# Splitting each projection and FFN matmul into two 64-row halves that sum outside TensorE

## The reference

```python
# attention half (16 heads of 64; Wf is 64x64)
n = LN(x)
q, k, v = n @ Wq, n @ Wk, n @ Wv
qf, kf = relu(q @ Wf + bf), relu(k @ Wf + bf)        # per head
kv, k_sum = einsum('blhf,blhd->bhfd', kf, v), kf.sum(axis=1)
out = einsum('blhf,bhfd->blhd', qf, kv) / maximum(einsum('blhf,bhf->blh', qf, k_sum), 1e-6)
x = x + LN(out @ Wo + bo)
# FFN half (1024 -> 4096 -> 4096 -> 4096 -> 1024, ternary weights, a scale per output row)
n = LN(x)
h = silu(n @ w1.T * s1) * (n @ w2.T * s2)
h = gelu(h @ h1.T * sh1)
h = gelu(h @ h2.T * sh2)
x = x + LN(h @ w3.T * s3)
```

## Time and profile before

| what | value |
|---|---|
| median of 3 runs | 8166.21 us (8165.4 to 8902.82) |
| profiled execution, its own time | 8160.16 us |
| span of the profiled execution, slowest of 8 cores | 8158.5 us (cores: 8137.2 to 8158.5) |
| mean granted TensorE clock, by core | 0.848 to 0.850 |
| TensorE matmuls busy | 5912.7 us (72%), 26064 instructions |
| TensorE weight loads busy | 2567.9 us (31%) |
| VectorE busy | 1504.9 us (18%) |
| ScalarE busy | 1102.5 us (14%) |
| chain that ended last, by engine | PE 69%, DVE 15%, DMA 8%, ACT 4%, issue 3% |

### The profile page before, as it was taken

How to read it: one execution, slowest core, us unless ns; L and a number is a source line. 1 busy time by engine, 2 the same in 40 slices (tenths; PEclk the granted TensorE clock), 3 DMA queues, 4 the chain that set the end, 5 groups by cost and what they waited for, 6 DMA issues and landing times.

```text
span 8158.5 us, 65823 instructions; the slowest of 8 cores (8137.2 to 8158.5 us)
## 1 busy us (share of the span) xinstructions
PE 5912.7 (72%) x26064; PEld 2567.9 (31%) x26064; DVE 1504.9 (18%) x1968; ACT 1102.5 (14%) x1781; POOL 214.0 (3%) x392
## 2 busy tenths in 40 slices
PE   3433336799996679999734333368999967799996
PEld 1211112344442334444312111123444423344442
DVE  2355541000002100000133555410000021000002
ACT  1221111110101111001112211111101011100011
POOL 0000000000000000000000000000000000000000
PEclk7666668899998889999866666688999978899998
DMA  3121102244443224344331211022444432344442
GB/s 68 31 57 31 36 26 48 56 78 75 75 78 85 55 57 78 73 77 78 72 78 31 57 32 36 26 52 56 75 77 78 79 91 44 60 78 73 77 78 78
DMA packets 106236, 507.70 MB, mean 62 GB/s; under 512 B 7568, under 2 KB 24016, under 8 KB 56784
## 3 DMA queue, kind: packets, MB, share of 16 engines
q0 software_dynamic: 76368, 402.82, 26.9%
q1 hardware_dynamic: 29568, 100.67, 3.4%
HBM read 864.23 MB, written 41.94 MB: 111 GB/s over the span
## 4 chain that ended last, share of the span: by engine, by line
PE 69%; DVE 15%; DMA 8%; ACT 4%; issue 3%; DVEq 0%; POOL 0%; ACTq 0%; SPq 0%; POOLq 0%
PE psb L56 69%; DMA wc<-w_t 5%; DVE ltmp L75 5%; DVE normsb L103 3%; DVE xa L75 2%; DVE vsb L103 2%; ACT sq L64 1%; DMA xbf<-x 1%; ACT kftm L64 1%; ACT z L64 1%; DVE xp L75 1%; DVE outt L75 1%; DVE rbc L96 1%; DVE y L75 1%; DMA xnw<-xn_hbm 0%
## 5 line engine op out<-in xcount | busy, mean ns | idle before, releaser
L56 PE MATMUL psb<-a,wc 128*128 128x512 bf16 x10240 | 2225.2, 381 | 47.8 <-DMA wc<-h_t 35.0
L56 PE MATMUL psb<-b,wc 128*128 128x512 bf16 x8192 | 1768.7, 379 | 4.8 <-ACT b L64 4.8
L56 PEld LDWEIGHTS psb<-a,wc 128*128 128x128 bf16 x10240 | 1004.2, 98 | 1268.7 <-issue 70.7
L56 PE MATMUL psb<-xnw,wc 128*128 128x512 bf16 x4096 | 963.2, 401 | 503.1 <-DMA wc<-w_t 388.1
L56 PEld LDWEIGHTS psb<-b,wc 128*128 128x128 bf16 x8192 | 801.3, 98 | 972.3 <-issue 6.7
L96 DVE COPY msb<-psb 1x512 f32<-1x512 f32 x40 | 27.1, 679 | 4609.7 <-PE psb L56 4553.4
L56 PEld LDWEIGHTS psb<-xnw,wc 128*128 128x128 bf16 x4096 | 416.1, 102 | 1051.8 <-issue 618.6
L89 DVE SCALAR_TENSOR_TENSOR a<-psb,s,ltmp 128x512 bf16<-128x512 f32 x256 | 192.2, 751 | 1214.0 <-PE psb L56 1195.0
L56 PE MATMUL psb<-xa,WA 128*128 128x512 bf16 x1024 | 251.9, 412 | 208.1 <-DVE xa L75 208.1
L64 ACT ACTIVATE a<-psb,sh 128x512 bf16<-128x512 f32 x256 | 175.9, 687 | 1597.7 <-PE psb L56 1597.7
L64 ACT ACTIVATE b<-psb,sh 128x512 bf16<-128x512 f32 x256 | 175.9, 687 | 1562.0 <-PE psb L56 1561.9
(11 more groups left out here) (79 smaller groups left out, 2324.2 us busy)
## 6 DMA issues: line engine op xcount, KB each, us to landing
wc<-h_t POOLq DMA_DIRECT2D x256, 1024.0 KB, 7.9
wc<-w_t POOLq DMA_DIRECT2D x96, 1024.0 KB, 9.4
xb<-x SPq DMA_DIRECT2D x16, 2048.0 KB, 9.8
xbf<-x POOLq DMA_DIRECT2D x16, 1024.0 KB, 8.9
xp_hbm<-xp SPq DMA_DIRECT2D x8, 2048.0 KB, 9.8
xpr<-xp_hbm SPq DMA_DIRECT2D x8, 2048.0 KB, 15.2
out<-outt SPq DMA_DIRECT2D x8, 2048.0 KB, 7.3
xn_hbm<-xa SPq DMA_DIRECT2D x8, 1024.0 KB, 3.9
```

What stands on the lines that cost most here:

```text
L56: ins = self.h.matmul(out, lhsT, rhs, start=start, stop=stop)
```

## The change

A new helper `mm2` issues two matmuls in place of one: rows 0 to 63 of the weights and of the moving data into one bank, with the array position (0, 0), and rows 64 to 127 into another bank, with the position (64, 0). It replaces `mm` in all projections (K, V, Q, output, W1, W2, H1, H2, W3). Each group of accumulating matmuls then leaves two partial sums in two banks (A and B), which are added on the way out: ACT copies bank A into a scratch tile in SBUF, DVE adds bank B to it. A new 128 x 512 float32 scratch tile `ltmp3` is placed, and the arena grows from 202 to 206 KB; all 8 banks serve as pairs. New waits keep the single scratch tiles from being overwritten (`st["l3_ve"]`, `st["ltmp_ve"]`), TensorE waits for DVE in place of ACT after K and Q, and `ln_fm` gets a wait for DVE on its source.

```diff
+    def mm2(self, outA, outB, lhsT, rhs, start, stop, sem=None):
+        ins = None
+        if self.E == "T":
+            self.h.matmul(outA, lhsT[0:64, :], rhs[0:64, :], start=start,
+                          stop=stop, tile_position=(0, 0))
+            ins = self.h.matmul(outB, lhsT[64:128, :], rhs[64:128, :], start=start,
+                                stop=stop, tile_position=(64, 0))
         self._inc(ins, sem, 1)
...
# K projection (the Q projection alike, V with its own views)
-            p.act(kql[oc], ps[bk][:, :], AF.Copy)
-            bank_consumed(bk, "se")
+            p.w("S", "ve", st["l3_ve"])
+            p.act(t["ltmp3"][:, :], ps[bA][:, :], AF.Identity)
+            bank_consumed(bA, "se")
+            se_i = p.c["se"]
+            p.w("V", "se", se_i)
+            p.tt(kql[oc], t["ltmp3"][:, :], ps[bB][:, :], ALU.add)
+            st["l3_ve"] = p.c["ve"]
+            bank_consumed(bB)
         se_k = p.c["se"]
+        ve_k = p.c["ve"]
+        p.w("T", "ve", ve_k)
...
# output projection
-            p.act(zl[oc], ps[bk][:, :], AF.Identity, bias=t["bo_t"][:, oc:oc + 1])
-            p.act(t["sq"][:, oc * TT:(oc + 1) * TT], ps[bk][:, :], AF.Square,
+            p.w("S", "ve", st["l3_ve"])
+            p.act(t["ltmp3"][:, :], ps[bA][:, :], AF.Identity,
                   bias=t["bo_t"][:, oc:oc + 1])
...
+            p.tt(zl[oc], t["ltmp3"][:, :], ps[bB][:, :], ALU.add)
...
+            p.w("S", "ve", ve_z)
+            p.act(t["sq"][:, oc * TT:(oc + 1) * TT], zl[oc], AF.Square)
...
# W1/W2 stage, one group
-                bw1 = h
-                bw2 = 2 + h
+                w1A, w1B = (0 + 2 * h, 1 + 2 * h)
+                w2A, w2B = (4 + 2 * h, 5 + 2 * h)
...
                 p.w("S", "pe", pe_w1)
                 p.w("S", "ve", st["ltmp_ve"])
-                p.act(t["ltmp"][:, :], ps[bw1][:, :], AF.Silu,
+                p.act(t["ltmp2"][:, :], ps[w1A][:, :], AF.Identity)
+                bank_consumed(w1A, "se")
+                se_i1 = p.c["se"]
+                p.w("V", "se", se_i1)
+                p.tt(t["ltmp3"][:, :], t["ltmp2"][:, :], ps[w1B][:, :], ALU.add)
+                bank_consumed(w1B)
+                ve_s1 = p.c["ve"]
+                p.w("S", "ve", ve_s1)
+                p.act(t["ltmp"][:, :], t["ltmp3"][:, :], AF.Silu,
                       scale=t["s1"][:, oc:oc + 1])
...
+                p.w("S", "pe", pe_w2)
+                p.act(t["ltmp2"][:, :], ps[w2A][:, :], AF.Identity)
+                bank_consumed(w2A, "se")
+                se_i2 = p.c["se"]
                 p.w("V", "pe", pe_w2)
-                p.w("V", "se", se_t1)
-                p.stt(al(oc, h), ps[bw2][:, :], t["s2"][:, oc:oc + 1],
+                p.w("V", "se", se_i2)
+                p.tt(t["ltmp3"][:, :], t["ltmp2"][:, :], ps[w2B][:, :], ALU.add)
+                bank_consumed(w2B)
+                p.stt(al(oc, h), t["ltmp3"][:, :], t["s2"][:, oc:oc + 1],
                       t["ltmp"][:, :], ALU.mult, ALU.mult)
...
# H1 and H2 stages
-                p.act(dstf(oc, h), ps[bk][:, :], AF.Gelu, scale=t[sc_t][:, oc:oc + 1])
+                p.w("S", "ve", st["ltmp_ve"])
+                p.act(t["ltmp"][:, :], ps[bA][:, :], AF.Identity)
...
+                p.tt(t["ltmp2"][:, :], t["ltmp"][:, :], ps[bB][:, :], ALU.add)
...
+                p.w("S", "ve", st["ltmp_ve"])
+                p.act(dstf(oc, h), t["ltmp2"][:, :], AF.Gelu,
+                      scale=t[sc_t][:, oc:oc + 1])
...
# W3 stage
+            p.act(t["ltmp"][:, :], ps[bA][:, :], AF.Identity,
+                  scale=t["s3"][:, oc:oc + 1])
...
+            p.stt(fl(oc, h), ps[bB][:, :], t["s3"][:, oc:oc + 1], t["ltmp"][:, :],
+                  ALU.mult, ALU.add)
```

More of the change, by code:

```diff
@@ L417, in emit_seq @@
         for oc in range(NCH):
-            bk = oc % 2
-            bank_wait(bk)
+            bA, bB = (0, 1) if oc % 2 == 0 else (2, 3)
+            bank_wait(bA)
+            bank_wait(bB)
             for ic in range(NCH):
[L421 to L424, removed]
+                p.mm2(ps[bA][:, :], ps[bB][:, :],
+                      t["WA"][:, ic * D + oc * 128: ic * D + (oc + 1) * 128],
+                      xal[ic], start=(ic == 0), stop=(ic == NCH - 1),
+                      sem="pe" if ic == NCH - 1 else None)
@@ L431, in emit_seq @@
+        p.w("T", "ve", ve_k)
         p.w("T", "dwB", st["wB_val"])
         for sub in range(4):
-            pair = (2, 3) if sub % 2 == 0 else (4, 5)
+            pairs = ((0, 1), (2, 3)) if sub % 2 == 0 else ((4, 5), (6, 7))
             for vh in range(2):
-                bk = pair[vh]
-                bank_wait(bk)
+                bA, bB = pairs[vh]
+                bank_wait(bA)
+                bank_wait(bB)
                 for ic in range(NCH):
[L438 to L441, removed]
-                pe_v = p.c["pe"]
-                p.w("V", "pe", pe_v)
+                    p.mm2(ps[bA][:, :], ps[bB][:, :],
+                          xal[ic][:, sub * 128:(sub + 1) * 128],
+                          t["WB"][:, ic * D + vh * 512: ic * D + (vh + 1) * 512],
+                          start=(ic == 0), stop=(ic == NCH - 1),
+                          sem="pe" if ic == NCH - 1 else None)
+                pe_v = p.c["pe"]
+                p.w("S", "pe", pe_v)
+                p.w("S", "ve", st["l3_ve"])
+                p.act(t["ltmp3"][:, :], ps[bA][:, :], AF.Identity)
+                bank_consumed(bA, "se")
+                se_i = p.c["se"]
+                p.w("V", "se", se_i)
@@ L534, in emit_seq @@
         for oc in range(NCH):
-            bk = oc % 2
-            bank_wait(bk)
+            bA, bB = (0, 1) if oc % 2 == 0 else (2, 3)
+            bank_wait(bA)
+            bank_wait(bB)
             for ic in range(NCH):
[L538 to L541, removed]
+                p.mm2(ps[bA][:, :], ps[bB][:, :],
+                      t["WA"][:, ic * D + oc * 128: ic * D + (oc + 1) * 128],
+                      xal[ic], start=(ic == 0), stop=(ic == NCH - 1),
+                      sem="pe" if ic == NCH - 1 else None)
             pe_q = p.c["pe"]
             p.w("S", "pe", pe_q)
-            p.act(kql[oc], ps[bk][:, :], AF.Copy)
-            bank_consumed(bk, "se")
-        se_q = p.c["se"]
+            p.w("S", "ve", st["l3_ve"])
+            p.act(t["ltmp3"][:, :], ps[bA][:, :], AF.Identity)
+            bank_consumed(bA, "se")
+            se_i = p.c["se"]
+            p.w("V", "se", se_i)
+            p.tt(kql[oc], t["ltmp3"][:, :], ps[bB][:, :], ALU.add)
+            st["l3_ve"] = p.c["ve"]
+            bank_consumed(bB)
+        ve_q = p.c["ve"]
+        p.w("T", "ve", ve_q)
         qfl = [t["qf"][:, c * TT:(c + 1) * TT] for c in range(NCH)]
         for c in range(NCH):
-            bk = 2 + c % 2
+            bk = 4 + c % 2
             bank_wait(bk)
-            p.w("T", "se", se_q)
             p.mm(ps[bk][:, :], t["wfbd"][:, :], kql[c], start=True, stop=True, sem="pe")
@@ L690, in emit_ffn_window @@
             for h in range(NH):
[L691 to L693 removed]
+                w1A, w1B = (0 + 2 * h, 1 + 2 * h)
+                w2A, w2B = (4 + 2 * h, 5 + 2 * h)
+                bank_wait(w1A)
+                bank_wait(w1B)
                 for ic in range(NCH):
[L695 to L698, removed]
+                    p.mm2(ps[w1A][:, :], ps[w1B][:, :],
+                          b1[:, ic * 512 + ocl * 128: ic * 512 + ocl * 128 + 128],
+                          xn_rhs(ic, h), start=(ic == 0), stop=(ic == NCH - 1),
+                          sem="pe" if ic == NCH - 1 else None)
                 pe_w1 = p.c["pe"]
[L700 removed]
+                bank_wait(w2A)
+                bank_wait(w2B)
                 for ic in range(NCH):
[L702 to L705, removed]
+                    p.mm2(ps[w2A][:, :], ps[w2B][:, :],
+                          b2[:, ic * 512 + ocl * 128: ic * 512 + ocl * 128 + 128],
+                          xn_rhs(ic, h), start=(ic == 0), stop=(ic == NCH - 1),
+                          sem="pe" if ic == NCH - 1 else None)
                 pe_w2 = p.c["pe"]
```

87 lines of the change are left out of this document (55 added, 32 removed).

## The result

The changed kernel takes 1.0359 times as long as the kernel before, with a 95% interval of 1.0337 to 1.0382: 8458 to 8465 us where the kernel before took 8164 to 8177.

A forecast was written before the change was run, and what follows sets the result against it. TensorE was taken to bound the kernel, mostly in the FFN. Terms 53 + 138 + 5 + 13 + 11 + 4 + 64 = 288 us on 8160.16 gave 8448 us; range for 8 in 10 runs 8,200 to 8,950.

The forecast's parts named there:

- attention: Both passes, 8 tiles each: later hand-overs between K, V and Q and a longer output projection chain add 64 us.
- W3's end: Behind W3, 4 times: the added evacuation steps take 0.17 + 0.75 + 0.15 more, 4 us.
- the 2.6 ns a pair: Outside W1/W2: a second matmul's leftover on each of 20,480 pairs adds 53 us, 0 if it overlaps.
- the chain of W1/W2: Six serial ACT and DVE steps, 4.96 us a group, bound the slab: 4.3 us longer each, 138 us.
- the prediction's two signs of being wrong: A pair costing more than 0.22 us, or the W1/W2 chain not being what ends last inside a slab.
- Pairs side by side: All split matmuls: both halves run concurrently in different array rows and banks, a pair taking 215.9 ns before any second leftover.
- late weights: Rival: the second half's weight load cannot be made ahead, giving about 9,600 to 10,600 us; chance 0.09.
- Hand-overs in the FFN: H1 to H2 and H2 to W3, 8 times: 1.64 us longer waits, 13 us, plus 11 us for a fallen clock.
- One after the other: Rival: the halves do not overlap, 5306 us more and about 13,500 us in all; chance 0.14.
- Table loads: Rival in W1/W2: Silu and Identity need different tables, + 590 us, 9,040 in all; chance 0.02.
- A clock fallen in W1/W2: Rival: TensorE's rests lower the clock, some 7.5 us a slab, 240 us, 8,690 in all; chance 0.10.
- Not slower: Rival: within 2% (163 us) if the W1/W2 chain is 4.6 us or less; chance 0.06.

The follow-up runs named there:

- squares_early: Changed kernel, with ScalarE's squares behind W3 waiting for tile f's last VectorE write, not the first layernorm's end: 8435.9 to 8443.5 us, ratio 1.0336.
- halves_in_turn: Changed kernel, with a group's 32 first halves in H1 and H2 issued before its 32 second halves instead of alternating: 11,311 us in one execution.
- deeper_weights_halves: Changed kernel with two more weight buffers in W1/W2, so a slab's loads run under the previous slab's matmuls: 8255.7 and 8256.1 us.
- output_pipelined: Changed kernel, output projection with two scratch tiles in turn and each Square after the next group's copy from bank A: 8422.9 and 8425.6 us, ratio 1.0318.

## Where the prediction was right, and which of its steps failed

- **The sum.** 8448 us was forecast, 288 above the execution it was built on; the changed kernel took 8458 to 8465, 292 to 299 more. The ratio of 1.0359 stands against 1.035. That total is partly luck: the 53 us for the pairs were not there, and W1/W2, attention and W3's end together cost some 72 us more than their terms.
- **The steps that failed** are three terms of the sum: the 2.6 ns a pair (53 us forecast, 0 measured), attention (64 forecast, 103 to 108 measured), and W3's end (4 forecast, some 20 measured). The main mechanism, the chain of W1/W2, was right, and neither of the prediction's two signs of being wrong appeared: a pair costs 0.216 us, under 0.22, and the chain is what ends last inside a slab.
- **Pairs side by side** ("I take side by side"): right. The second half starts mostly 12 to 21 ns behind the first at the full clock, more than the 4 ns of the page "TensorE: Matmul & The Clock Gate" (Part 3) of the Trainium skill, whose concurrency the trace confirms: it costs nothing, since the pairs still follow one another every 0.216 us. The step "with 2.6 ns more a pair for the leftover of a second matmul" failed: the two leftovers overlap, and at the full clock a pair takes 215.8 ns in H1, H2 and W3, to a hundredth of a nanosecond what a whole matmul takes. The end of its range at 0 was the right value. In W3 the halves even came out 3 us shorter in all, by shorter waits for weights. (For late weights fully exposed the prediction's own numbers give some 10,460, not 10,600.)
- **The W1/W2 chain**: right in place and in size. 4.96 us a group was forecast, 4.88 measured: ScalarE's copy out of PSUM as Identity without a scale took 0.597 us, not 0.687, and Silu from SBUF 0.722, not 0.63. A slab grew by 4.3 us, as forecast (34.0 - 29.7). The stage grew by 154 and not by 143, because the gaps for loads grew too, which no term had.
- **Hand-overs in the FFN**: the wait grew by 1.8 us where 1.64 was forecast, 14.7 us against 13. "Between the two I take half" gave 11 us for a fallen clock: it fell at 6 of the 8 hand-overs of this core, for 8.4 us, and for 10 us on the average of the cores. That term was close; its two parts were not, since it fell more often than in half of the cases and cost 1.7 us and not 2.7.
- **Attention**: 64 us were forecast, and 103 are found tile by tile, of the 108 in the table. In pass 1 a tile grew by 3.5 us (2.9 forecast), with the 2.1 us between K and V as foreseen. In pass 2 it grew by 9.4 us (5.1 forecast): Q and its hand-over 2.0 for 0.95, the output projection up to the statistics 4.5 for 4.1, the statistics themselves 1.8 for 0, and the rest of the tile 1.1 for 0. The failed step is "Behind it stands the layernorm's statistics, which wait for the squares, so all of it is on the path": true, but it priced the delay alone and not what follows at another clock. The gap before the statistics went from 1.8 to 3.8 us, and their 16 matmuls from 3.2 to 5.0. Of the last 1.1 us, 0.7 are the statistics of the tile's next layernorm (5.6 us from first to last start where they took 4.9).
- **W3's end**: 4 us forecast, some 20 found, and this step failed too. The added wait before the squares names the last VectorE step at the time of emission; in the second turn of the loop that is the end of the first tile's layernorm. The prediction counted the new steps behind W3 and overlooked this wait. squares_early gives back 20 us.
- **Rivals.** One after the other: what it would cost is real, as halves_in_turn shows (+ 0.174 us a pair), but not what happens. Late weights: no pair in a dense stretch shows them. Table loads: 13 before and after, so Silu's set has Identity. A clock fallen in W1/W2: inside a slab it stayed full, even at 77% busy in deeper_weights_halves. Not slower: a chain of 4.6 us was needed and it is 4.88.

## What to carry to other kernels

In this kernel, splitting a matmul that already fills the array's rows bought nothing at best, and turned one step of evacuation into two; look for its price where evacuation is a chain, not in the matmuls. To price a chain, write down every link, the engines' own order among them, and compare its length with TensorE's time for the group; a stage that waits for loads hides the difference, so such a price is only as small as that wait is long. When a step moves the end of a burst by a few microseconds, price what comes next at the lower clock too, and look at more than the first matmul behind the gap, since the clock can fall a few matmuls later. Read every added wait with the value it has in the second turn of its loop.

## What was not expected of the hardware

- A half with 64 rows takes 0.216 us when it stands alone, as a whole matmul does, and two in different row groups share that time, with mostly 12 to 21 ns between their starts at the full clock.
- In halves_in_turn four pairs overlapped at every border between first and second halves, so the row groups seem to run up to four matmuls ahead of each other.
- ScalarE's Identity from PSUM to SBUF took 0.597 us without and 0.687 us with a bias or scale tile; with the scale tile and an SBUF source Silu and Gelu took 0.722.
- How often the clock was at the lower level behind a gap, over all eight cores: behind 1.2 us between FFN stages at none of 64, behind 1.8 us before the statistics (kernel before) at none of 64, behind 2.8 us there (output_pipelined) at 54 of 64, behind 3.0 to 3.3 us between FFN stages at 55 of 64, behind 3.8 us before the statistics at 63 of 64. Gaps of 0.4 to 0.9 us in W1/W2, one after another for 310 us, left it full. Between FFN stages the clock often fell only after the first few matmuls of the new stage, and which hand-over was spared differed from core to core.
